# Null value as an offset of the values, small turned weights copied first, and the last stage's shared input normalised by ScalarE

## The reference

```
x = x + ffn0(cond0(x, cond_64))      # cond0: MoE, 8 experts top-2 + shared; ffn0: MoE, 16 experts top-4 + shared
x = x + ffn1(cond1(x, cond_64))      # cond1: attention; ffn1: MoE, 8 experts top-2, 128 -> 512 -> 128
```

```
# cond0: logits of the router
logits = (x @ wt.T + repeat(cond_64 @ wg.T)) / 2

# cond1 (b = 32, n = 32, 16 heads of 64): null_kv = cond_64, one extra key and one extra value
k = concat([null_kv[0], k]);  v = concat([null_kv[1], v])
attn = softmax(l2norm(q) @ l2norm(k).T * 8 + bias, masked)     # 33 keys, the null key among them
out  = layernorm(concat_heads(attn @ v) @ Wout) * g_out

# ffn1: the experts share one normalised input
logits = out @ router_W + router_b
xhat   = (out - mean(out)) * rsqrt(var(out) + 1e-5)
y_e    = gelu((xhat * ln_g[e] + ln_b[e]) @ W1[e] + b1[e]) @ W2[e] + b2[e]
```

## Time and profile before

| | us |
|---|---|
| median of three runs | 267.24 |
| the profiled execution, whole | 269.58 |
| its span, first to last instruction | 267.8 |
| TensorE matmul busy in the span | 250.1 (93%) |
| VectorE busy | 214.1 (80%) |
| ScalarE busy | 148.0 (55%) |
| GpSimd busy | 104.8 (39%) |
| mean granted TensorE clock, share of full | 0.986 |

### The profile page before, as it was taken

One profiled execution on the slowest core, in us unless ns is written; L12 is line 12 of the kernel. 1 busy time (PEld: TensorE's weight loads), 2 busy tenths in 40 slices (PEclk: granted clock), 3 DMA queues, 4 the chain that ended last, 5 costly groups with the idle time before them and its releaser, 6 DMA issues.

```text
span 267.8 us, 5239 instructions
## 1 busy us (share of the span) xinstructions
PE 250.1 (93%) x1888; PEld 201.5 (75%) x1888; DVE 214.1 (80%) x433; ACT 148.0 (55%) x248; POOL 104.8 (39%) x146
## 2 busy tenths in 40 slices
PE   6899999889999978979999998989899999999994
PEld 5786548667899967868868766868688888888884
DVE  7477867997878298887679886989998888788883
ACT  1456614335550446688435455396687867877550
POOL 2897510132484546843447666533140101101000
PEclk9589999999999999999999999999999999999999
DMA  6993150010200001210310000007093000000002
GB/s 172 236 274 46 52 225 0 1 43 0 41 12 0 2 5 47 71 39 5 85 38 2 4 2 2 0 2 234 21 305 111 2 1 0 0 2 0 1 0 80
DMA packets 25033, 14.51 MB, mean 54 GB/s; under 512 B 11824, under 2 KB 21717, under 8 KB 25008
## 3 DMA queue, kind: packets, MB, share of 16 engines
q1 hardware_dynamic: 24464, 13.89, 19.2%
q0 software_dynamic: 544, 0.29, 0.7%
HBM read 13.55 MB, written 0.62 MB: 53 GB/s over the span
## 4 chain that ended last, share of the span: by engine, by line
PE 70%; DVE 20%; issue 3%; ACT 3%; POOL 2%; DVEq 0%; POOLq 0%; ACTq 0%
PE ps L939 13%; PE ps L941 13%; PE ps L940 13%; PE ps L1106 5%; PE ps L1275 3%; PE ps L1036 3%; PE ps L1195 3%; PE ps L1263 3%; PE ps L1063 3%; PE ps L1000 2%; PE ps L1161 2%; DVE g_lo L1806 1%; PE ps L964 1%; DVE arena L1427 1%; DVE arena L1520 1%
## 5 line engine op out<-in xcount | busy, mean ns | idle before, releaser
L939 PE MATMUL ps<-act_hi,w_hi 128*128 128x512 f32 x120 | 48.9, 407 | 2.0 <-DVE arena L1520 1.0
L878 ACT ACTIVATE att_bias<-ps,bias 128x512 f32<-128x512 f32 x64 | 43.5, 689 | 13.0 <-PE ps L941 11.7
L941 PE MATMUL ps<-act_hi,w_lo 128*128 128x512 f32 x120 | 47.5, 396 | 0.0
L940 PE MATMUL ps<-act_lo,w_hi 128*128 128x512 f32 x120 | 47.4, 395 | 0.0
L1806 DVE TENSOR_TENSOR g_lo<-att_bias,g_hi 128x1024 fp32r<-128x1024 f32 x32 | 40.0, 1259 | 0.6
L939 PEld LDWEIGHTS ps<-act_hi,w_hi 128*128 128x128 f32 x120 | 22.9, 191 | 8.1 <-issue 3.4
L941 PEld LDWEIGHTS ps<-act_hi,w_lo 128*128 128x128 f32 x120 | 22.8, 190 | 5.1
L940 PEld LDWEIGHTS ps<-act_lo,w_hi 128*128 128x128 f32 x120 | 23.0, 192 | 4.5
L1802 DVE CAST g_hi<-att_bias 128x1024 fp32r<-128x1024 f32 x16 | 12.4, 775 | 8.3 <-ACT att_bias L878 8.3
L707 ACT ACTIVATE xc<-ps 128x512 f32<-128x512 f32 x18 | 10.8, 597 | 14.8 <-PE ps L941 14.8
L1477 DVE TENSOR_TENSOR arena<-arena,ps 128x512 f32<-128x512 f32 x24 | 16.1, 684 | 3.4 <-PE ps L1000 3.2
(11 more groups left out here) (293 smaller groups left out, 591.7 us busy)
## 6 DMA issues: line engine op xcount, KB each, us to landing
arena<-gate_m SPq DMA_DIRECT2D x16, 256.0 KB, 5.2
w_stage<-in_L_ffn_W SPq DMA_DIRECT2D x9, 256.0 KB, 2.6
w_stage<-in_L_ffn_W SPq DMA_DIRECT2D x1, 1792.0 KB, 8.1
x_tok<-in_x SPq DMA_DIRECT2D x2, 256.0 KB, 3.2
w_stage<-in_L_ffn_w_gate SPq DMA_DIRECT2D x1, 512.0 KB, 5.1
w_stage<-in_L_ffn_w_up SPq DMA_DIRECT2D x1, 512.0 KB, 6.7
w_stage<-in_L_cond_Wq SPq DMA_DIRECT2D x1, 512.0 KB, 6.4
f_down<-in_L_ffn_w_down SPq DMA_DIRECT2D x1, 512.0 KB, 6.1
```

Source lines behind the costliest of these rows:

```text
L878: act.activation(gelu[:, k % 2, b, :], bank(b), ACT.Gelu, bias=bias1[:, c:c + 1])\
L939: pe.matmul(dst, wh, xh, start=first, stop=False)
L940: pe.matmul(dst, wh, xl, start=False, stop=False)
L941: return pe.matmul(dst, wl, xh, start=False, stop=last)
```

## The change

The null value is subtracted from all value rows by GpSimd before the loop over tiles, and added back as a bias when ScalarE copies the attended values out of PSUM. That replaces `null_rows`, `null_values`, `p_null`, `null_turn`, `null_turned` and the last two instructions of `project`. One more small load (`nv_row`) is issued by SyncE after `nv_col`. Three memsets of GpSimd are gone.

VectorE copies the first turned half, then the two small turned weights, then the second half; the two `gate_sel` copies move from ahead of these to behind `cond_rows`.

`input_normed` moves from VectorE to ScalarE, as an ACTIVATE with scale and bias read from two columns; ScalarE runs it ahead of `att_turned(t)` and, for the last two tiles, ahead of `route_tanh(0)` and of `gelu_high(0)`. The bias is made by GpSimd: `both_rstd` gets two more small operations, one ahead of the power and one behind it, and signals after the last.

```diff
+            pool.wait_ge(ld["att"], 176)
+            for s in range(HALVES):
+                pool.wait_ge(act_v, s + 1)
+                v = v_tok[:, s * HT:(s + 1) * HT, :]
+                pool.tensor_tensor(v, v, nv_row[:, :].unsqueeze(1).broadcast_to([P, HT, DH]), ALU.subtract)\
+                    .then_inc(pool_v, 1)
...
             def both_rstd(t):
...
                 link(pool.tensor_tensor(var2[:, t, 1:2], var2[:, t, 1:2], mv_g[:, t, 1:2], ALU.add))
-                pool.tensor_tensor(rstd2[:, t, :], var2[:, t, :], half_neg[:, 0:2], ALU.pow).then_inc(pool_rstd, 1)
+                link(pool.tensor_tensor(shift2[:, t, :], mv_g[:, t, 0:1], minus[:, 0:1], ALU.mult))
+                link(pool.tensor_tensor(rstd2[:, t, :], var2[:, t, :], half_neg[:, 0:2], ALU.pow))
+                pool.tensor_tensor(shift2[:, t, :], shift2[:, t, :], rstd2[:, t, 1:2], ALU.mult).then_inc(pool_rstd, 1)
...
-                               ACT.Copy).then_inc(act_attT, 1)
+                               ACT.Identity, bias=nv_col[:, 0:1]).then_inc(act_attT, 1)
...
+            def input_normed(t):
+                act.wait_ge(pool_rstd, t + 1)
                 if t >= 2:
-                    act.wait_ge(pe_wo, t - 1)
-                act.activation(pn_T[0:HEADS, t % 2, :], bank(7)[0:HEADS, 0:P], ACT.Copy).then_inc(act_pn, 1)
+                    act.wait_ge(pe_xcT, t - 1)
+                act.activation(xh_tok[:, t % 2, :], xc[:, t, :], ACT.Identity, scale=rstd2[:, t, 1:2],
+                               bias=shift2[:, t, :]).then_inc(act_xn, 1)
...
             for t in range(TILES):
+                if t >= 2:
+                    input_normed(t - 2)
                 att_turned(t)
-                null_turned(t)
...
+            input_normed(TILES - 2)
             route_tanh(0)
             gelu_block(0, 0)
             gelu_block(0, 1)
             out_turned(TILES - 2)
             gelu_block(0, 2)
             gelu_block(0, 3)
+            input_normed(TILES - 1)
             gelu_high(0)
...
                 for b in range(HB):
-                    pe.matmul(bank(6)[:, 0:P], att_T[:, t % 2, b, :], w_out[:, b, :], start=(b == 0), stop=False)
-                pe.matmul(bank(6)[:, 0:P], pn_T[:, t % 2, :], nv_out[:, :], start=False, stop=True).then_inc(pe_wo, 1)
+                    mm = pe.matmul(bank(6)[:, 0:P], att_T[:, t % 2, b, :], w_out[:, b, :],
+                                   start=(b == 0), stop=(b == HB - 1))
+                mm.then_inc(pe_wo, 1)
...
-            for s in range(HALVES):
-                dve.wait_ge(pe_xT, s + 1)
-                turned(s, bank(4 + s), 0, lo=False)
+            dve.wait_ge(pe_xT, 1)
+            turned(0, bank(4), 0, lo=False)
             dve.wait_ge(pe_small, 1)
             dve.tensor_copy(wt_T[:, 0:C_EXP], bank(7)[:, 0:C_EXP]).then_inc(v_small, 1)
             dve.tensor_copy(cond_wg_T[:, :], bank(7)[0:DH, 64:64 + SEQ + C_EXP]).then_inc(v_small, 1)
+            dve.wait_ge(pe_xT, 2)
+            turned(1, bank(5), 0, lo=False)
             first_low(0)
```

More of the change, by code:

```diff
@@ L152, in two_layers @@
         rstd2 = sb("rstd2", [P, TILES, 2])
+        shift2 = sb("shift2", [P, TILES, 1])
+        minus = sb("minus", [P, 1])
         std = sb("std", [P, TILES])
@@ L1093, in turn_tiles @@
                 mm.then_inc(pe_xT, 1)
[L1095 to L1102, removed]
             def down_tile(s, t, b, first, last):
@@ L1221, in _ @@
                     turn_keys(1)
[L1222 to L1230, removed]
-                    pe.wait_ge(act_xhT, t - 2)
-                if t == TILES - 1:
-                    pe.wait_ge(act_lg, 1)
-                pe.transpose(bank(7)[0:HEADS, 0:P], p_null[:, t % 2, :], ident[:, :]).then_inc(pe_pn, 1)
             def out_turn(t):
-                pe.wait_ge(act_pn, min(t + 3, TILES))
                 if t >= 1:
                     pe.wait_ge(act_xhT, t)
+                else:
+                    pe.wait_ge(act_kd, 3)
                 pe.wait_ge(v_wo, t + 1)
                 pe.transpose(bank(7)[:, 0:P], xc[:, t, :], ident[:, :])
-                pe.wait_ge(v_xh, t + 1)
+                pe.wait_ge(act_xn, t + 1)
                 pe.transpose(bank(7)[:, P:2 * P], xh_tok[:, t % 2, :], ident[:, :]).then_inc(pe_xcT, 1)
@@ L1312, in _ @@
                 values(t)
-                null_turn(t)
                 if t == 0:
@@ L1392, in _ @@
             dve.wait_ge(ready, 1)
-            for g in (0, LOW_ROW):
-                dve.tensor_copy(gate_sel[g:g + F_EXP, :, :].rearrange("p q (h m) -> p (q h) m", h=2),
-                                ident[g:g + F_EXP, g:g + F_EXP].unsqueeze(2).broadcast_to([F_EXP, F_EXP, DH]))\
-                    .then_inc(v_sel, 1)
             dve.tensor_reduce(seq_tile[:, :], ident[0:SEQ, 0:SEQ].rearrange("p (t q) -> p t q", q=BPT), AX, ALU.add)
@@ L1421, in _ @@
                 .then_inc(v_small, 1)
+            for g in (0, LOW_ROW):
+                dve.tensor_copy(gate_sel[g:g + F_EXP, :, :].rearrange("p q (h m) -> p (q h) m", h=2),
+                                ident[g:g + F_EXP, g:g + F_EXP].unsqueeze(2).broadcast_to([F_EXP, F_EXP, DH]))\
+                    .then_inc(v_sel, 1)
             def c_unit(u):
@@ L1579, in _ @@
             rp_norm(1)
-            dve.wait_ge(ld["att"], 160)
-            dve.wait_ge(ready, 9)
+            dve.wait_ge(ld["att"], 176)
             for u in range(8, 16):
                 f_unit(u)
-                if u == 8:
-                    for h in range(2):
-                        rows = slice(h * DH, (h + 1) * DH)
-                        dst = nv_sel[rows, :, :].rearrange("p b h -> p (b h)")[:, h:h + 18 * 7 + 1:18]
-                        ins = dve.tensor_copy(dst, nv_col[rows, 0:1].broadcast_to([DH, HB]))
-                    ins.then_inc(v_nv, 1)
                 if u == 9:
@@ L1779, in _ @@
                     scored(t + 2)
-                if t >= 2:
-                    input_normed(t - 2)
                 if t + 1 < TILES:
```

48 lines of the change are left out of this document (11 added, 37 removed).

## The result

| | before | after |
|---|---|---|
| median, us | 267.10 (266.1 to 267.93, 4 runs) | 271.01 (270.14 to 272.06, 4 runs) |
| ratio, 95% interval | | 1.0149 [1.0097, 1.0201] |
| profiled execution: span, us | 267.8 | 269.9 |
| mean granted clock of TensorE | 0.986 | 0.986 |

The change makes the kernel 3.9 us slower; 1.8 us faster was forecast, and the time lies above the range. From profile to profile the span grows by only 2.1 us, because the profiled execution of before was a long one for its kernel (2.5 us above the 267.10, that of after 1.05 above its median). Throughout, a median takes all executions, and a ratio compares only those within 1.5% of their kernel's fastest.

What follows compares the result with a forecast made beforehand. TensorE was taken as the bound, with a VectorE-GpSimd loop only 0.41 us shorter that would bind after the change. Start -2.0 and the rest +0.2 gave -1.8 us: 267.24 to 265.4, range 262.9 to 267.9.

Steps and rivals of the forecast that it cites:

- Part 3, the loop: Attention's loop over tiles: GpSimd's two added operations cost 0.55 us a tile, making the step 5.25 us.
- second loop: Chain `projected`, GpSimd's `both_rstd` and `probs`, VectorE's turned probabilities: 4.70 us a tile before, against TensorE's 5.11.
- Rival (c): GpSimd's two additions cost as much as the power, 1.38 us a tile: 271.2 us; chance 0.08.
- Part 3, the tail: End of attention: `m_down(0)` about 0.3 us late, mostly absorbed before `m_down(2)`; +0.2 us carried, between 0 and +0.8.
- Part 2: Attention, null work off TensorE: `values(0)` 0.98 us earlier, `projected(0)` 1.45 earlier, TensorE's own tile step 0.35 shorter.
- Part 1: Start, copies reordered: small product 0.97 us earlier, idle down to 0.4; gain taken as 2.0 us, between 1.05 and 3.7.
- rival (a): TensorE's clock stays high at the start, which then gains 3.7 us: 263.7 us in all; chance 0.20.

Runs made afterwards that it cites:

- pair_unused: Changed kernel with normalisation back on VectorE but GpSimd's two added small operations kept, their result unread: 269.98 us, ratio 1.0117.
- late_fixed: Changed kernel, GpSimd's added pair behind the next tile's `probs` (late tiles: behind `both_rstd`), VectorE waiting for the last `both_rstd` before copying gelus: 268.33 us, ratio 1.0050.
- tail_wait: Changed kernel with one more wait: VectorE waits for GpSimd's last `both_rstd` before it copies the first gelus: 269.54 us, ratio 1.0086.
- null_fill: Kernel before with only the null-value change and the filler, four unused 128-column TensorE products ahead of `values(0)`: 265.71 us, ratio 0.9940.
- start_only: Kernel before with only the reordered VectorE copies at the start: 266.39 us, ratio 0.9973.
- norm_only: Kernel before with only the normalisation moved to ScalarE and GpSimd's two added small operations: 273.00 us, ratio 1.0208.
- tail_order: Changed kernel with ScalarE's `gelu_high(0)` put ahead of the last `input_normed`: 271.13 us, ratio 1.0127.
- casts_late: Changed kernel with normalisation back on VectorE, no added pair, `gate_sel` copies moved behind `c_unit(5)` and `c_unit(6)`: 269.52 us, ratio 0.9942 over five of twelve executions.
- both_repairs: Changed kernel, normalisation on VectorE, no pair, four unused products before `values(0)`, `gate_sel` copies behind `c_unit(5)` and `c_unit(6)`: 269.52 us, ratio 0.9879 over two of six executions.

## Why the prediction was wrong

**Part 3, the loop: right.** "The second loop's step is then 4.70 + 0.55 = 5.25": 5.19 to 5.26. The pair costs 0.52 in place of 0.55, pair_unused shows it by itself, and with the pair moved (late_fixed, with the two orders that move with it) the loop takes 24.03, against 23.57 without the pair. So the place in GpSimd's order was what cost. Rival (c), the pair as dear as the power, fell in the loop; that its 271.2 us is near the measured 271.0 is chance, as the steps are not its own.

**Part 3, the tail: the step that failed most.** "VectorE's `input_normed(7)`, which is gone, so `m_down(0)` comes at about +0.3. TensorE's wait of 0.77 before `m_down(2)` takes up most of it". That was +0.2 us at the end, with 0.3 already lost at `projected(5)`, so -0.1 for the tail; it is +2.3. I had the row that says it: `input_normed` at 1.27 us in place of 0.34 where GpSimd works beside it. I read it as VectorE's loss and didn't ask what VectorE's next instructions do to GpSimd. The wait I took away was what kept the two apart. The last `both_rstd` was to cost the pair's 0.55 more; it cost 1.85 more (3.35 us for 1.50), with ScalarE's `gelu_high(0)` and TensorE's last turn behind it. tail_wait shows it: with the wait put back, 1.9 us of 2.3 are gone in the trace and 1.5 in the time (0.2 of the 1.9 comes ahead of `projected(7)` and may be the clock, whose second fall came before `projected(5)` there).

The page GPSIMD Engine Reference of the Trainium skill (Specifications) names this as well: GpSimd's SBUF interfaces are shared with VectorE, with contention from VectorE's instructions in a two-port mode or with two SBUF inputs. The traces agree: the power ran 1.69 us beside the copy of the gelus and the subtraction with two SBUF inputs, 0.69 without them. I cited that page for the 1.27 us and took no price from it for GpSimd.

**Part 2: right in time, wrong in clock.** `values(0)` was to come 0.98 us earlier and `projected(0)` 1.45. Count from TensorE's last turn of the queries at a wait, first before, then after:

```profile
119.94 1.06 PE L1161 MATMUL ps<-ident,arena 128*128 128x128 f32 x8 [1.25 <-ACT arena L758]
```

```profile
117.98 1.06 PE L1153 MATMUL ps<-ident,arena 128*128 128x128 f32 x8 [1.25 <-ACT arena L760]
```

Then `values(0)` is 10.04 - 9.04 = 1.00 earlier. But `projected(0)` is 0.3 later. Of the 1.8 us missing, 1.6 are the clock's (9.51 for 7.93 behind `values(0)`). I asked what the clock would do at the start only, and put no price on the idle stretch that I had myself forecast ahead of `values(0)`: 1.81 us of products gone, 0.98 of them won. With the filler it is 133.48 - 116.69 = 16.8 in null_fill, and 138.17 - 119.94 - 1.45 = 16.8 was forecast.

**Part 1: its gain belongs to one execution.** The small product came with 0.4 us of idle before it, and the clock was high at the start of after, as rival (a) had it, who put 3.7 on that. Between the two marks above it is 3.1 us less than in before. But the first mark itself came 1.0 later (it lies between 5.75 and 6.88 us over the traces), so up to the attention after leads by 119.94 - 117.98 = 1.96, for the 2.0 forecast: a hit by luck, rival (a)'s start less a later first mark. Then "the profiled run is 2.3 us above the median; I take the difference over as it is" carried it to the median, where most executions have a mean clock of 0.994 or 1.000 and not 0.986. start_only measures 1.35 between the medians, with a ratio of 0.9973 that can't be told from 1. The 0.97 us of the earlier product isn't passed on.

**The sum again.** From trace to trace the terms close: start -1.96 for -2.0, `projected(0)` +0.3 for -1.45, loop +1.5 for +1.7, tail +2.3 for -0.1. That is +2.1 for -1.8, and +2.1 is what the span grew by. The medians differ by 3.9. Of the 1.8 us between, 0.4 lies outside the span, for which I had no term: time less span is 1.74 to 1.87 us in every execution of the kernels without the pair, 2.04 to 2.13 in norm_only and pair_unused, and 2.12 to 2.23 in after and the kernels made from it with ScalarE's `input_normed`. What makes it so the profile doesn't show. The other 1.4 is that the profiled execution of before lies 2.5 us above its median and that of after 1.05. It may be the clock: 0.986 in the profiled execution of before, which most others don't have, but 0.985 to 0.992 in all four of after, and in the profiled one it falls a second time behind TensorE's waits in the loop. No experiment was made for that second fall alone.

## What to carry to other kernels

A wait that is removed may have been a fence between two engines that slow each other: before taking it away, look at what its engine does next, and beside whom. A small operation costs by its place in a loop between engines, not by its work: find the loop's return path, and put it behind the hand-over (and then follow every instruction that it is moved past). Where work is taken from TensorE and something else holds its next instruction, price the clock behind the idle stretch, and set the profiled execution's clock beside that of the median before carrying a gain over.

## What the runs showed of the hardware

- TensorE fell to 1.2 GHz for 3.4 us after an idle stretch of 0.68 us that stood among small products; four unused products of 128 columns in that place kept it at 2.4 GHz, in six traces of six. Without them eight of nine fell, and tail_order, with the same 0.68 us, did not. The length of the idle stretch alone doesn't decide it: 1.25 us ahead of the last turn of the queries led to no fall in any of the 18 traces, 1.66 to 1.68 us near 98 us led to one in five of the 18, and at the start 1.35 us led to one in before, while 1.14 in null_fill led to none.
- VectorE and GpSimd slow each other, in both directions and far beyond double: GpSimd's power of two columns 0.69 to 1.69 us, its multiplication of one column 0.19 to 1.20, VectorE's 16x1024 copy 0.68 to 3.57.
- GpSimd's 17 DMA issues at the start hold its queue for 9.1 us (11.38 to 20.52 in before, 0.5 each). Beside them VectorE's copy took 0.74 us in casts_late and 1.27 in both_repairs.
- A kernel with the pair on GpSimd takes 0.3 to 0.4 us more outside its span, first to last instruction, than one without, in every execution.
